# A factorization machine with a small network behind it: four slots in place of three, an end in two blocks, narrow products for the layers

## The reference

```python
B, N_DIMS, EMBED_DIM = (1024, 12500, 16)
H1, H2 = (128, 64)
x_reg = input_data @ W_lin.T + b_lin
emb = input_data @ factors
sum_squared = jnp.square(emb.sum(axis=1))
squared_sum = (jnp.square(input_data) @ jnp.square(factors)).sum(axis=1)
h = jax.nn.relu(emb @ W1.T + b1)
h = jax.nn.relu(h @ W2.T + b2)
dnn_out = h @ W3.T + b3
x = x_reg + 0.5 * (sum_squared - squared_sum)[:, None] + dnn_out
x = 0.5 + jax.nn.sigmoid(x) * 5.0
```

## Time and profile before

| | before |
|---|---|
| median of 3 runs | 141.37 us |
| the profiled execution | 140.98 us, of which the span is 138.5 us |
| PE, PEld busy | 107.4 (78%), 30.1 (22%) |
| DVE, ACT, POOL busy | 52.7 (38%), 65.4 (47%), 16.1 (12%) |
| read from HBM | 52.16 MB, 377 GB/s over the span |
| chain of waits | DMA 56%, PE 35% |

### The profile page before, as it was taken

One profiled execution on the slowest core, in us unless ns is written; L12 is line 12 of the kernel. 1 busy time (PEld: TensorE's weight loads), 2 busy tenths in 40 slices (PEclk: granted clock), 3 DMA queues, 4 the chain that ended last, 5 costly groups with the idle time before them and its releaser, 6 DMA issues.

```text
span 138.5 us, 2597 instructions
## 1 busy us (share of the span) xinstructions
PE 107.4 (78%) x1014; PEld 30.1 (22%) x1014; DVE 52.7 (38%) x48; ACT 65.4 (47%) x70; POOL 16.1 (12%) x53
## 2 busy tenths in 40 slices
PE   6088976792997887696799699487696788799991
PEld 1022111120221121121113222021111112146760
DVE  0392253150452254045222735055135225447441
ACT  4032473370672474266353867075357247456712
POOL 4024110100031100100110205100101000000000
PEclk9999999999599999999999999999999999999998
DMA  4999999999999999999999987999999999999000
GB/s 138 402 394 426 435 421 426 435 416 426 440 416 388 435 416 435 440 412 435 426 421 435 431 241 322 421 435 426 431 435 431 431 431 412 416 408 362 28 5 1
DMA packets 4581, 52.24 MB, mean 377 GB/s; under 512 B 520, under 2 KB 652, under 8 KB 1504
## 3 DMA queue, kind: packets, MB, share of 16 engines
q1 hardware_dynamic: 4576, 52.16, 90.5%
HBM read 52.16 MB, written 0.00 MB: 377 GB/s over the span
## 4 chain that ended last, share of the span: by engine, by line
DMA 56%; PE 35%; issue 2%; DVE 2%; SPq 2%; ACT 1%; DVEq 0%; ACTq 0%
DMA xr<-in_x_groups 56%; PE p_lin L443 28%; PE p_tot L443 2%; PE p_last L443 2%; PE p_h L515 1%; DVE sq L367 1%; PE p_h L535 1%; ACT sg L298 1%; PE p_h L520 1%; SPq L199 0%; DVE h L392 0%; SPq L197 0%; SPq L196 0%; SPq L195 0%; ACT lin L284 0%
## 5 line engine op out<-in xcount | busy, mean ns | idle before, releaser
L273 ACT ACTIVATE sq<-xr 128x1536 f32<-128x1536 f32 (+1 forms) x44 | 53.4, 1262 | 54.1 <-DMA xr<-in_x_groups 54.1
L367 DVE TENSOR_TENSOR sq<-xr 128x1536 f32<-128x1536 f32 x22 | 38.7, 1762 | 64.8 <-DMA xr<-in_x_groups 64.7
L443 PE MATMUL p_lin<-xr,wr 128*17 128x512 f32 x352 | 43.5, 612 | 20.2 <-DMA xr<-in_x_groups 20.2
L443 PE MATMUL p_lin<-sq,wz 128*18 128x512 f32 x352 | 42.4, 599 | 2.1 <-DVE sq L367 1.2
L443 PEld LDWEIGHTS p_lin<-xr,wr 128*17 128x17 f32 x352 | 9.2, 98 | 52.4 <-issue 50.3
L443 PEld LDWEIGHTS p_lin<-sq,wz 128*18 128x18 f32 x352 | 9.3, 98 | 35.1 <-ACT sq L273 18.6
L236 POOL COPY wr<-hd 128x136 f32 (+1 forms) x22 | 8.6, 391 | 55.2 <-PE p_lin L443 55.2
L239 POOL COPY wz<-s_all 128x8 f32 (+1 forms) x22 | 5.2, 236 | 29.6 <-PE p_lin L443 29.6
L443 PE MATMUL p_lin<-xf,hd 128*17 128x512 f32 x4 | 3.6, 1046 | 3.9 <-DMA xf<-in_x_first 3.9
L373 DVE TENSOR_TENSOR sq<-xe 128x1024 f32<-128x1024 f32 (+2 forms) x5 | 4.8, 956 | 2.7 <-DMA xe<-in_x_end 2.6
L280 ACT ACTIVATE sq<-xe 128x1024 f32<-128x1024 f32 (+3 forms) x7 | 4.9, 719 | 1.7 <-DMA xe<-in_x_end 1.6
(11 more groups left out here) (54 smaller groups left out, 40.6 us busy)
## 6 DMA issues: line engine op xcount, KB each, us to landing
xr<-in_x_groups SPq DMA_DIRECT2D x22, 2048.0 KB, 10.5
xe<-in_x_end SPq DMA_DIRECT2D x2, 1024.0 KB, 13.7
xe<-in_x_end SPq DMA_DIRECT2D x3, 512.0 KB, 16.4
hd<-in_head SPq DMA_DIRECT2D x1, 934.0 KB, 4.9
xf<-in_x_first SPq DMA_DIRECT2D x1, 512.0 KB, 6.0
xe<-in_x_end SPq DMA_DIRECT2D x1, 384.0 KB, 17.7
xl<-in_x_rest SPq DMA_DIRECT2D x1, 336.0 KB
xe<-in_x_end SPq DMA_DIRECT2D x1, 128.0 KB, 17.5
```

The costliest lines, as they stand in the source:

```text
L273: nc.scalar.activation(sq[:, s, c:c + n, :], xr[:, s, c:c + n, :], ACT.Square).then_inc(act_squared, 1)
L367: nc.vector.tensor_tensor(sq[:, s, 0:BY_DVE, :], xr[:, s, 0:BY_DVE, :], xr[:, s, 0:BY_DVE, :], ALU.mult).then_inc(dve_squared, 1)
L443: return nc.tensor.matmul(out, lhsT, rhs, start=False, stop=False, skip_group_check=True)
```

## The change

- `RING` is 4: four slots of `xr`, `sq`, `wr`, `wz`. `xe` is gone: the end's data lies in the four slots of `xr` and its squares in those of `sq`. The SBUF that they take together stays the same.
- The end has 32 chunks in place of 16, so half 1 has 8 groups (12 to 19), and its blocks have 384 and 128 columns. Its ten pieces wait for the slot they lie in (`last_slot`).
- The products of layers 1 and 2 are cut into four of 32 output rows, in four column tiles.
- The loops start at group 0 and have four groups a turn; nothing is left over. `sq_used` starts at 4. POOL's loops are nested, with the slot as a variable, and both its copies wait for `sq_used`; `x_used` is gone.
- The squares of the last block have a bank of their own, `p_sq`.

```diff
-RING = 3
-ENDS = 16
+RING = 4
+ENDS = 32
...
-BLOCKS = ((0, 512), (512, 256), (768, 128), (896, 128))
-PIECES = ((1, 0, 8, 4), (1, 8, 8, 4), (2, 0, 8, 4), (2, 8, 8, 4), (3, 0, 8, 2), (3, 8, 6, 6), (3, 14, 2, 2))
+BLOCKS = ((0, 512), (512, 384), (896, 128))
+PIECES = ((1, 0, 8, 4), (1, 8, 8, 4), (1, 16, 8, 4), (1, 24, 6, 3), (1, 30, 2, 1),
+          (2, 0, 8, 4), (2, 8, 8, 4), (2, 16, 8, 4), (2, 24, 6, 6), (2, 30, 2, 2))
...
-        xe = sb("xe", [P, ENDS * HALF])
...
+        xe = xr[:, :].rearrange("p s c b -> p (s c b)")
+        sq_end = sq[:, :].rearrange("p s c b -> p (s c b)")
+        def last_slot(i):
+            k, c, n, _ = PIECES[i]
+            return (ENDS * (BLOCKS[k][0] - HALF) + (c + n) * BLOCKS[k][1] - 1) // (CHUNKS * HALF)
...
-            def load(g, s):
-                sp.wait_ge(sq_used, g - RING + 1)
-                sp.dma_start(xr[:, s].rearrange("p c b -> p (c b)"),
-                             x_groups[bass.ds(g, 1)].rearrange("g p n -> (g p) n")).then_inc(x_landed[s], 16)
-            with sp.Fori(1, TOTAL // RING) as r:
+            with sp.Fori(1, sum(ROUNDS)) as r:
                 for s in range(RING):
-                    load(RING * r + s, s)
-            for s in range(LEFT):
-                load(TOTAL - LEFT + s, s)
+                    sp.wait_ge(sq_used, RING * r + s + 1)
+                    sp.dma_start(xr[:, s].rearrange("p c b -> p (c b)"),
+                                 x_groups[bass.ds(RING * r + s, 1)].rearrange("g p n -> (g p) n")
+                                 ).then_inc(x_landed[s], 16)
             at = 0
             for i, (k, c, n, _) in enumerate(PIECES):
                 rows = x_end[at:at + P * n * width(i)].rearrange("(p m) -> p m", p=P)
+                sp.wait_ge(sq_used, TOTAL + last_slot(i) + 1)
                 sp.dma_start(piece(xe, i, c, n), rows).then_inc(end_landed[i], 16)
...
+            def place(g, s, at):
+                pool.wait_ge(sq_used, g + 1)
+                nc.gpsimd.tensor_copy(wr[:, bass.ds(s, 1), :, :].rearrange("p s c k -> p (s c) k"),
+                                      w[:, bass.ds(at, CHUNKS), :]).then_inc(wr_ready, 1)
+                nc.gpsimd.tensor_copy(wz[:, bass.ds(s, 1), :, LIN:WZ].rearrange("p s c k -> p (s c k)"),
+                                      s_all[:, bass.ds(at, CHUNKS)]).then_inc(wz_ready, 1)
+            with pool.Fori(0, ROUNDS[0]) as r:
+                with pool.Fori(0, RING) as s:
+                    place(RING * r + s, s, 1 + CHUNKS * (RING * r + s))
...
-            act.wait_ge(sq_used, TOTAL - LEFT)
-            square_end(0)
-            square_end(1)
-            square_end(2)
+                    squares(r, s)
+            for i in range(6):
+                square_end(i)
             act.wait_ge(p_lin_done[1], 1)
             copy_lin(1, 0)
             copy_lin(1, 1)
-            square_end(3)
-            nc.scalar.copy(rest[:, :], p_lin[1][:, HALF // 2:HALF]).then_inc(rest_copied, 1)
             layer1(1)
-            square_end(4)
+            nc.scalar.copy(rest[:, :], p_lin[1][:, BLOCKS[1][1]:HALF]).then_inc(rest_copied, 1)
+            square_end(6)
+            square_end(7)
             embedding_square(1)
-            square_end(5)
-            square_end(6)
+            square_end(8)
+            square_end(9)
...
+                mm = clear(ps[:, :])
+            mm.then_inc(sq_used, RING)
...
+            def first_layer(bank, n, rhs):
+                for t in range(4):
+                    mm = nc.tensor.matmul(bank[32 * t:32 * t + 32, 0:n], pr[:, C_W1 + 32 * t:C_W1 + 32 * t + 32], rhs,
+                                          start=True, stop=True, skip_group_check=True)
                 return mm
...
-                    nc.tensor.matmul(p_h1[u][:, 0:BLOCKS[k][1] // 2], pr[:, C_W1:C_W1 + H1], lin[:, part(k, u)],
-                                     start=True, stop=True).then_inc(p_h1_done[k], 1)
-            def layer1_whole(k, bank):
-                pe.wait_ge(lin_ready[k], 2)
-                nc.tensor.matmul(bank[:, 0:BLOCKS[k][1]], pr[:, C_W1:C_W1 + H1], lin[:, cols(k)],
-                                 start=True, stop=True).then_inc(p_h1_done[k], 1)
+                    first_layer(p_h1[u], BLOCKS[k][1] // 2, lin[:, part(k, u)]).then_inc(p_h1_done[k], 1)
...
-                for u in range(2):
-                    mm = nc.tensor.matmul(p_h2[u * H2:(u + 1) * H2, row(k)], pr[:, C_W2:C_W2 + H2], h1[:, part(k, u)],
-                                          start=True, stop=True)
+                for t in range(4):
+                    mm = nc.tensor.matmul(p_h2[32 * t:32 * t + 32, row(k)],
+                                          pr[:, C_W2 + t % 2 * 32:C_W2 + t % 2 * 32 + 32], h1[:, part(k, t // 2)],
+                                          start=True, stop=True, skip_group_check=True)
...
+            for i in range(3):
+                multiply_end(i)
+                add_squares_end(i)
             multiply_end(3)
-            add_squares_end(2)
+            multiply_end(4)
+            add_squares_end(3)
+            add_squares_end(4).then_inc(p_lin_done[1], 1)
+            multiply_end(5)
             layer1(1)
-            multiply_end(4)
-            add_squares_end(3).then_inc(p_lin_done[2], 1)
+            multiply_end(6)
+            add_squares_end(5)
             terms(1)
-            multiply_end(5)
             pe.wait_ge(h1a_ready[1], 1)
             pe.wait_ge(h1b_ready[1], 1)
             layer2(1)
-            multiply_end(6).then_inc(p_lin_done[3], 1)
-            layer1_whole(2, p_h1[0])
-            pe.wait_ge(lin_ready[3], 2)
-            add_squares_end(4, P)
-            layer1_whole(3, p_h1[1])
+            multiply_end(7)
+            add_squares_end(6)
+            embedding_square(1)
+            multiply_end(8)
+            layer3(1).then_inc(p_tot_done[1], 1)
+            multiply_end(9).then_inc(p_lin_done[2], 1)
+            add_squares_end(7)
+            pe.wait_ge(lin_ready[2], 1)
+            first_layer(p_h1[0], BLOCKS[2][1], lin[:, cols(2)]).then_inc(p_h1_done[2], 1)
+            add_squares_end(8)
+            add_squares_end(9).then_inc(squares_done, 1)
             pe.wait_ge(sg_ready[0], 1)
             terms(2)
             pe.wait_ge(h1b_ready[2], 1)
             layer2(2)
-            add_squares_end(5, P)
-            add_squares_end(6, P).then_inc(squares_done, 1)
-            embedding_square(1)
-            layer3(1).then_inc(p_tot_done[1], 1)
-            pe.wait_ge(h1b_ready[3], 1)
-            layer2(3)
-            pe.wait_ge(sg_ready[1], 1)
-            terms(3)
             embedding_square(2)
-            layer3(2).then_inc(p_tot_done[2], 1)
             pe.wait_ge(qs_ready, 1)
             for u in range(2):
-                add_mm(tot_bank(3)[64 + 32 * u:65 + 32 * u, row(3)], pr[:, C_SX:C_SX + 1], qs[:, 64 * u:64 * (u + 1)])
-            embedding_square(3)
-            layer3(3).then_inc(p_tot_done[3], 1)
```

More of the change, by code:

```diff
@@ L214, in _ @@
                 rows = x_end[at:at + P * n * width(i)].rearrange("(p m) -> p m", p=P)
+                sp.wait_ge(sq_used, TOTAL + last_slot(i) + 1)
                 sp.dma_start(piece(xe, i, c, n), rows).then_inc(end_landed[i], 16)
                 at += P * n * width(i)
-            for k in range(2):
+            for k in range(3):
                 sp.wait_ge(y_ready[k], 1)
                 sp.dma_start(out[cols(k)].rearrange("(u b) -> u b", u=2), y[64:P:32, row(k)]).then_inc(y_stored, 16)
[L221 to L224, removed]
             sp.wait_ge(y_stored, 48)
@@ L245, in _ @@
             nc.gpsimd.tensor_copy(ws[:, 0, LIN:WZ], s_all[:, 0:1]).then_inc(ws_ready, 1)
[L246 to L247 removed]
             nc.gpsimd.tensor_copy(ws[:, 1:ENDS + 1, LIN:WZ].rearrange("p c k -> p (c k)"),
                                   s_all[:, W_END:ALL]).then_inc(ws_ready, 1)
[L250 to L252 removed]
+            def place(g, s, at):
[7 more added lines that the diff above has]
+                    place(RING * r + s, s, 1 + CHUNKS * (RING * r + s))
             with pool.Fori(0, ROUNDS[1]) as r:
[L254 to L257, removed]
+                with pool.Fori(0, RING) as s:
+                    place(GROUPS + RING * r + s, s, 1 + CHUNKS * (RING * r + s))
         @block.scalar
@@ L264, in _, with squares @@
             nc.scalar.activation(sqf[:, :], xf[:, :], ACT.Square).then_inc(first_squared, 1)
[L266 to L270, removed]
+            def squares(r, s):
+                act.wait_ge(x_landed[s], 16 * (r + 1))
+                act.wait_ge(sq_used, RING * r + s + 1)
                 c = BY_DVE
@@ L299, in sigmoid @@
                                      bias=bias[64:P, :]).then_inc(sg_ready[k], 1)
-            for s in range(RING):
-                squares(s, 0, s, False)
-            with act.Fori(1, ROUNDS[0]) as r:
+            with act.Fori(0, ROUNDS[0]) as r:
                 for s in range(RING):
-                    squares(RING * r + s, r, s, True)
```

(47 more changed lines are left out.)

84 lines of the change are left out of this document (30 added, 54 removed).

## The result

| | before | changed |
|---|---|---|
| median | 141.23 us (141.07 to 141.82, 4 runs) | 136.37 us (136.26 to 136.72, 4 runs) |
| ratio | | 0.9653 (95% interval 0.9618 to 0.9687) |
| the profiled execution | 140.98, span 138.5 | 136.26, span 134.2 |
| HBM read | 52.16 MB, 377 GB/s | 52.16 MB, 389 GB/s |

What follows compares the result with a forecast made beforehand. The arrival of bytes was taken to set the end for 128 of 138.5 us, then the tail. 140.98 - 2.1 (fourth slot) - 1.9 (tail) = 137.0; median 0.39 above gives 137.4, stated as 137.3 us, range 135.5 to 140.0.

Steps and rivals of the forecast that it cites:

- Fourth slot: Transfers after group 12: a slot more on order removes the hole, 2.1 us off every later landing (1.1 to 2.4).
- the hole: Slices 24 and 25 at 241 and 322 GB/s; groups 14 and 15 land 7.04 us apart, 2.15 us lost.
- the step at group 4: Groups 3 and 4 land 6.43 us apart; one DMA engine 1.5 us behind, mostly explained by an instruction packet.
- Waits of the end's transfers, loops from group 0, POOL: End pieces waiting for slots with 10.6 us of cover, nested loops and POOL's copies: all covered, cost nothing.
- PE in the end: PE waits for data before wide pieces, ends the wide block at L - 3.1, takes the last piece at L + 1.5.
- L: The time at which the last transfer lands, from which the prediction counts the steps of the tail.
- Tail: From last landing to result: ready at L + 4.9 against 6.8 us before, so -1.9 us.
- Narrow products: Layers 1 and 2: each stay in wide products costs PE about 0.2 us, twice on the new path.
- The lateness moves: Rival in the landings: a late DMA engine stays late, another 1.5 us delay on it; 138.8 us, chance 0.17.
- Code fetched again at each branch: Rival in the loops: bodies of 275 instructions refetch code at branches, +6 us, 143 us; chance 0.05.
- The signs named: Trace signs: slices above 400 GB/s, groups 11 to 16 4.9 us apart, last landing near 127.5, span 134.5 to 135, PE pauses.

Runs made afterwards that it cites:

- experiment 1: The changed kernel with three slots in place of four and an end of 24 chunks in eight pieces: 138.71 us, ratio 0.9847.
- experiment 2: The kernel before, three slots, with ACT and DVE squaring group 12 ahead of half 0's sigmoid and scaling: 139.53 us, ratio 0.9893.
- experiment 4: The kernel before with only the products of layers 1 and 2 cut into four of 32 output rows: 140.61 us, ratio 0.9980.

## Why the prediction was right, point by point

- **Fourth slot, -2.1.** The number is right: 2.2 at the last landing, 2.3 to 2.7 in experiment 1. The mechanism is right too: that the hole came from the late release of group 12's slot is shown by experiment 2, and with four slots it is gone. The near agreement is partly luck, for two things that the term left out cancel. The hole's place gained 1.6 and not 2.15, since a step of 0.5 behind an instruction packet stands there now; and the step at group 4, which was to stay, fell from 1.5 to 0.7.
- **Waits of the end's transfers, loops from group 0, POOL: nothing.** Right as far as the rows go: no slice below 397 GB/s between the 4th and the 37th, the full pieces of 384 columns 3.6 to 3.8 us apart. With three slots the end's waits did cost (experiment 1).
- **PE in the end.** Near, though PE had less room than reckoned: it pauses ahead of two of the four wide pieces and from 120.5 us on no more. PE ended the wide block near L - 2.9 (last squares from 123.05, 1.49 long), where L - 3.1 was reckoned, and DVE's copy came at L + 2.0 (129.43), as summed.
- **Tail, -1.9.** Measured 2.0: ready at L + 4.9.
- **Narrow products.** Mis-sized: 0.2 a stay, twice on the path, was reckoned; without them the kernel loses 0.7, mostly because PE is behind, so that stays ahead of the last piece count too. In the profiles the tail is 5.7 us without them and 4.9 with them, so the other parts of the change shortened it by 1.2 and not by the 1.5 or more that were left for them: here too two errors cancel in the sum.
- **The lateness moves.** Its mechanism is there: steps of 0.7 and 0.5 us at groups 4 and 15, each behind an instruction packet, where before one of 1.5 and the hole stood. In sum no more lateness than before.
- **Code fetched again at each branch.** Fell: five packets, at 29.0, 82.7, 116.3, 126.0 and 129.8 us, and none at the later turns of a loop. The rule of two pages that the prediction quotes from the Trainium skill (Runtime: NRT & Kernel Launch, section Instruction fetch mechanics) led to no fetch in these loops of 275 instructions. Two blocks of 256 can hold such a loop, so the run does not refute the rule either.
- **The signs named.** The number of packets, the last landing near 127.5 and PEclk came as named, PE's pauses in part. Not met were 400 GB/s from the third slice on (385 there, 394 before), 4.9 us between all of groups 11 to 16 (5.40 at group 15) and, by 0.3 us, the span's 134.5.
- **The 0.9 us between 137.3 and 136.37.** The span was 0.3 shorter than its sum (134.5), the time outside the span 2.06 in place of the 2.48 carried over, and the median 0.11 over the profiled execution in place of some 0.3.

## What to carry to other kernels

Where transfers set the pace, look for the slices in which they stop, and find whose slot was released late. A fourth slot helps (2.3 us or more here), and so do a few lines of order ahead of the release (1.6 us). Behind the last byte, sum up what PE still has in its queue; where it has no pause, moving one product forward need not help (0.1 us here, within the scatter).

When a sum comes out right, compare its terms with the new trace as well: here the landings and the tail each held two misses that cancelled.

## What had not been expected of the hardware

A packet of instructions (16 KB, 1.0 to 1.1 us) beside data showed up as a step of 1.5, 0.7 or 0.5 us in the landings, or as none. The data packet of 16 KB behind it took 1.1 to 1.2 us in place of 0.61, and a sixth packet cost under 0.3 us of the whole.

PE's clock fell in one profile after an idle of 2.30 us and not in two others after 2.42 and 2.43.

The time outside the span differed between the versions: 2.48 and 2.36 us in the profiled executions of the kernel before and of experiment 4, 2.18 in experiment 2, 2.04 to 2.10 in the changed kernel and those with its end of 32 chunks, 1.78 in experiment 1. The last store holds two blocks in the kernel before and one in the changed kernel, but experiment 1 stores as the changed kernel does, so the store alone does not explain it. No run took it apart.
